# An attention block with a routed feed-forward layer on one core: the routing cut into three parts instead of two, and the attention step put in another sequence

## The reference

```python
xn = ln(x, g_norm)
q = (xn @ Wq).reshape(b, n, HEADS, DIM_HEAD).transpose(0, 2, 1, 3)
...
sim = jnp.einsum('bhid,bjd->bhij', l2norm(q) * q_scale, l2norm(k) * k_scale) * SCALE + attn_bias   # causal, masked
attn = jax.nn.softmax(sim, axis=-1)
out = jnp.einsum('bhij,bjd->bhid', attn, v)
y = ln(out.transpose(0, 2, 1, 3).reshape(b, n, HEADS * DIM_HEAD) @ Wout, g_out)
...
logits = y @ wr.T + rb
scores, idx = jax.lax.top_k(softmax(logits), 2)          # two of seven, weights normed to 1
out = expert(y, shared)
for e in range(7): out = out + w[..., e:e + 1] * expert(y, e)   # expert: (silu(y @ g.T) * (y @ u.T)) @ d.T
return x + out
```

## Time and profile before

| | us |
|---|---|
| median of 3 runs (433.98, 434.51, 672.77) | 434.51 |
| the profiled execution | 434.13 |
| its span, first to last instruction | 432.0 |
| PE, DVE, ACT, POOL busy | 357.3, 292.6, 279.5, 229.2 |
| a step of the attention, t = 3 to 14 | 12.04 |
| first send to the first routed tile's first matmul | 45.1 |
| first routed tile to the end of the span | 109.6 |

### The profile page before, as it was taken

The page is one execution under the profiler, slowest core; times in us unless marked ns, Lnnn a source line. Parts: engine busy times, 40 slices in busy tenths (PEclk is TensorE's granted clock), DMA queues, the critical chain, the costliest instruction groups (busy, mean ns, idle before and its releaser), DMA issues.

```text
span 432.0 us, 10178 instructions
## 1 busy us (share of the span) xinstructions
PE 357.3 (83%) x2921; PEld 295.1 (68%) x2922; DVE 292.6 (68%) x1144; ACT 279.5 (65%) x935; POOL 229.2 (53%) x253
## 2 busy tenths in 40 slices
PE   0286776999999999999998989697619999999980
PEld 0275655677777777777776648496519999999980
DVE  1848385888888888888889894757305565566545
ACT  1385594999999999999996773464304444444440
POOL 5024843678876667667872552277730444344420
PEclk9998995999999999999999687869958999999997
DMA  6726299990000000000000000011121222111117
GB/s 185 204 80 200 67 212 191 202 163 2 2 2 2 3 2 2 3 0 2 3 2 2 1 2 0 14 50 58 49 56 26 63 61 61 49 56 55 35 58 236
DMA packets 39479, 26.55 MB, mean 61 GB/s; under 512 B 4464, under 2 KB 37130, under 8 KB 39438
## 3 DMA queue, kind: packets, MB, share of 16 engines
q1 hardware_dynamic: 34256, 20.60, 21.8%
q0 software_dynamic: 2240, 4.23, 2.9%
q10 hardware_dynamic: 2942, 1.21, 1.1%
HBM read 12.89 MB, written 13.54 MB: 61 GB/s over the span
## 4 chain that ended last, share of the span: by engine, by line
PE 60%; DVE 16%; POOL 7%; issue 7%; ACT 5%; DMA 4%; SPq 1%; ACTq 0%; DVEq 0%; POOLq 0%
PE bank L1188 45%; PE bank L1185 14%; POOL sent_rows L537 7%; DVE p_space L1014 2%; ACT p_space L687 2%; DMA q_space<-in_L_cond_g_dram 2%; DVE biasm_space L1140 1%; DVE xn L934 1%; DMA bias<-result_rows 1%; DVE low L1018 1%; DVE p_space L841 1%; ACT xn L610 1%; DVE GL L918 1%; ACT yh L779 1%; DVE norm_in L812 1%
## 5 line engine op out<-in xcount | busy, mean ns | idle before, releaser
L687 ACT ACTIVATE p_space<-p_space,low 128x129 f32<-128x129 f32 x256 | 99.0, 391 | 6.4 <-DVE low L1018 6.4
L502 POOL TENSOR_TENSOR p_space<-p_space,inv 128x516 f32<-128x516 f32 x64 | 67.1, 1049 | 66.1 <-DVE inv L1026 66.1
L1014 DVE SCALAR_TENSOR_TENSOR p_space<-bank,rn,biasm_space 128x129 f32<-128x129 f32 x256 | 72.0, 343 | 22.3 <-PE bank L1188 22.0
L493 POOL TENSOR_TENSOR biasm_space<-bias,madd 128x516 f32<-128x516 f32 x64 | 75.6, 1192 | 7.4 <-DVE p_space L1014 7.3
L543 POOL DMA_INDIRECT result_rows<-oT_space,dest_ring x38 | 37.6, 990 | 60.8 <-DVE dest_ring L1154 60.1
L768 ACT ACTIVATE biasm_space<-bank 128x384 f32<-128x384 f32 x54 | 26.6, 492 | 58.1 <-PE bank L1185 58.0
L1185 PE MATMUL bank<-ident,p_space 128*128 128x128 f32 (+1 forms) x272 | 48.5, 297 | 2.4 <-POOL p_space L502 2.1
L687 ACT ACTIVATION_READ_ACCUMULATOR p_space<-p_space,low 128x1 f32 x256 | 48.5, 190 | 0.0
L1188 PE MATMUL bank<-DT,biasm_space 128*128 (+1 forms) x324 | 46.4, 281 | 1.2 <-ACT biasm_space L768 1.2
L702 ACT ACTIVATE pT<-bank 128x512 f32<-128x512 f32 x64 | 37.3, 583 | 13.9 <-PE bank L1188 12.8
L1018 DVE TENSOR_REDUCE low<-p_space 128x4 f32<-128x516 f32 x64 | 44.2, 691 | 2.2
(11 more groups left out here) (217 smaller groups left out, 705.4 us busy)
## 6 DMA issues: line engine op xcount, KB each, us to landing
sent_rows<-fill_row SPq DMA_DIRECT2D x2, 1950.0 KB, 24.1
sent_rows<-fill_row SPq DMA_DIRECT2D x2, 1885.0 KB, 19.6
q_space<-sent_rows SPq DMA_DIRECT2D x38, 65.0 KB, 1.9
xs<-in_x_dram SPq DMA_DIRECT2D x4, 256.0 KB, 6.3
bias<-bias_rows SPq DMA_DIRECT2D x1, 1024.0 KB, 5.8
xn<-result_rows SPq DMA_DIRECT2D x4, 256.0 KB, 4.4
bias<-result_rows SPq DMA_DIRECT2D x4, 256.0 KB, 5.6
out_dram<-xs SPq DMA_DIRECT2D x4, 256.0 KB, 2.5
```

The source lines that it names most:

```text
L493: nc.gpsimd.tensor_tensor(biasm[:, b % 2, heads, :], bias[:, heads, :], madd[:, b:b + 1, :].to_broadcast([P, HC, KEYS]), ALU.add).then_inc ...
L502: nc.gpsimd.tensor_tensor(v, v, spread(inv[:, b % 2, heads], KEYS), ALU.mult).then_inc(p_normed, 1)
L687: last = nc.scalar.activation(v, v, ACT.Exp, bias=low[:, b % 2, h:h + 1], accum_out=den[:, b % 2, h:h + 1])
L1014: last = nc.vector.scalar_tensor_tensor(Pb[:, q, h, :], src, rn[:, q, h:h + 1], biasm[:, q, h, :], ALU.mult, ALU.add)
```

## The change

1. The routing goes in three parts, of eight, four and four batches. Part 0 is normed in steps 13 and 14 and chosen, ranked and shared out in step 17; part 1 is normed in steps 15 and 16, chosen in step 17 and ranked in step 18; part 2 takes the place that the second part had among the tiles. `root_y` now runs three times instead of twice.
2. PE's step has another sequence: `mix(2)` moves from the end of a step to the next one, beside `mix(3)`; `scores(3)` moves up beside `scores(2)`; `turn_pn` goes ahead of `turn_p(3)`. The null key's matmul becomes 128 rows deep, with zeros in the 112 new rows (two more fills in the prologue).
3. The first `keep_oT` of a batch moves from ACT to DVE, between `invert(1, 1)` and `scores(3)`, and the next `mix` waits for it by a semaphore of its own. `keep_q(1)` changes places with `keep_pT(1)`, and `keep_pn` with `keep_pT(3)`, on ACT.
4. POOL's step has another sequence, with `add_mask` of chunks 3, 2 and 1 behind `norm_p(1)`.

```diff
-    PARTS = (range(0, Y_FIRST), range(Y_FIRST, NB))
+    PARTS = (range(0, NB - 8), range(NB - 8, NB - 4), range(NB - 4, NB))
...
@@ POOL, step
                 norm_p(2, 3)
-                add_mask(2, 2)
+                norm_p(3, 3)
+                norm_p(0, 2)
                 add_mask(0, 0)
-                norm_p(3, 3)
-                add_mask(3, 2)
-                norm_p(0, 2)
+                norm_p(1, 2)
+                add_mask(3, 1)
+                add_mask(2, 0)
                 add_mask(1, 0)
-                norm_p(1, 2)
...
-            pool.wait_ge(y_normed, Y_FIRST // 4)
-            nc.gpsimd.tensor_copy(send[0][0][:, :, 0:D], y_sb[:, 0:Y_FIRST, :]).then_inc(send_made[0][0], 1)
+            pool.wait_ge(y_normed, PARTS[0].stop // 4)
+            nc.gpsimd.tensor_copy(send[0][0][:, :, 0:D], y_sb[:, 0:PARTS[0].stop, :]).then_inc(send_made[0][0], 1)
...
@@ ACT, step
-                keep_oT(1, 3)
+                keep_oT()
...
+                keep_q(1)
                 keep_pT(1)
-                keep_q(1)
                 square_q(1)
...
+                if t == NB:
+                    keep_yT(0)
                 if t == NB + 1:
-                    for g in range(Y_FIRST // 4):
-                        keep_yT(g)
+                    stage(0, 1)
+                    keep_yT(2)
                 keep_pT(2)
+                if t == NB + 1:
+                    weigh(0)
                 exp(1, 1)
+                if t == NB:
+                    keep_yT(1)
                 keep_sums()
...
-                keep_oT(0, 2)
+                keep_pn()
                 keep_pT(3)
-                keep_pn()
...
@@ DVE, step
+                def keep_oT():
+                    if on(2):
+                        b = t - 2
+                        dve.wait_ge(mixed, NCH * b + 2)
+                        need(dve, y_made, b - 1)
+                        nc.vector.tensor_copy(oT[:, p, 0:HALF * P].rearrange("p (k s) -> p k s", k=HALF),
+                                              bank[6][:, :].rearrange("p (k s) -> p k s", k=HALF)[:, :, ::-1]).then_inc(oT0_kept, 1)
...
                 scores(0)
...
+                invert(3, 2)
                 scores(1)
-                invert(3, 2)
...
                 if t == NB + 1:
-                    dve.wait_ge(router_turned, 1)
...
-                if t == NB + 2:
                     choose(0)
                     mark(0)
                     rank(0)
                     share_out(0)
+                if t == NB + 2:
+                    rank(1)
+                    share_out(1)
                 keep_y()
+                if t == NB + 1:
+                    choose(1)
+                    mark(1)
...
+                keep_oT()
                 scores(3)
...
+                if t == NB - 3:
+                    root_y(0)
                 if t == NB - 2:
-                    gather_y(Y_FIRST - 1)
-                    root_y(0)
+                    scale_y(0)
+                    scale_y(1)
                 if t == NB - 1:
-                    scale_y(0)
+                    root_y(1)
                 if t == NB:
-                    scale_y(1)
                     scale_y(2)
...
@@ PE, step
+                if t == NB + 1:
+                    logits(0)
+                    logits(1)
                 if t == NB + 2:
-                    count(0)
+                    count(1)
                 queries(0)
                 turn_p(0)
+                mix(2, 3)
                 mix(3, 3)
...
                 project()
                 if t == NB + 1:
-                    for g in range(Y_FIRST // 4):
-                        logits(g)
+                    count(0)
+                    logits(2)
                 turn_p(2)
                 mix(0, 2)
                 scores(2, 1)
+                scores(3, 1)
                 mix(1, 2)
...
+                turn_pn()
                 turn_p(3)
-                scores(3, 1)
                 turn_sums()
...
-                turn_pn()
-                mix(2, 2)
```

More of the change, by code:

```diff
@@ L169, in rows_in_tile @@
             return tile[:, :, :].rearrange("p a b -> p (a b)")[:, 0:n * ROW].rearrange("p (b c) -> p b c", c=ROW)
-        send = ((rows_in_tile(bias, Y_FIRST), rows_in_tile(madd, Y_FIRST)),
-                (shared(p_space, 0, NB - Y_FIRST, ROW), shared(p_space, (NB - Y_FIRST) * ROW, NB - Y_FIRST, ROW)))
+        send = tuple(tuple(rows_in_tile(tile, PARTS[1].stop)[:, PARTS[k].start:PARTS[k].stop, :] for tile in (bias, madd))
+                     for k in range(2)) + (
+                tuple(shared(p_space, m * len(PARTS[2]) * ROW, len(PARTS[2]), ROW) for m in range(TOP)),)
         whole = (shared(p_space, H * KEYS + (NB + 1) * DH, 2, I), shared(biasm_space, (NB + 1) * 2 * DH, 2, I))
@@ L205, in adaln_ffn_kernel, with run_end @@
         placed = shared(o_space, 7 * NB * NE, TOP, NB, NE)
-        run_up = (shared(o_space, 9 * NB * NE, 2, PADS[0] + Y_FIRST, NE), shared(o_space, 12 * NB * NE, 2, PADS[1] + NB - Y_FIRST, NE))
+        RUNS = [2 * (PADS[k] + len(PARTS[k])) * NE for k in range(len(PARTS))]
+        run_up = tuple(shared(o_space, 9 * NB * NE + sum(RUNS[0:k]), 2, PADS[k] + len(PARTS[k]), NE) for k in range(len(PARTS)))
+        assert sum(RUNS) <= 4 * NB * NE
+        def run_end(k):
+            return run_up[k][:, SIDES[k], PADS[k] + len(PARTS[k]) - 1, :]
         tiles_up = shared(o_space, 13 * NB * NE, 2, EPAD + NE)
@@ L286, in run_steps, with logits_at, count_at @@
                 step(t, t % 2, lambda k, t=t: 0 <= t - k < NB)
[L288 to L294, removed]
+        y_bank = (4, 4, 2, 6)
+        def logits_at(k):
+            at = (3, 5, 6)[k], (2 * P, 0, 0)[k]
+            return bank[at[0]][:, at[1]:at[1] + NB * NE].rearrange("p (b e) -> p b e", b=NB)
+        def count_at(k, m):
+            first = (0, 0, 2 * P)[k] + m * P
+            return bank[(3, 3, 6)[k]][:, first:first + len(PARTS[k]) * NE]
         def turned_bank(t, c):
@@ L654, in keep_yT, with stage @@
                 nc.scalar.activation(YT[:, g * 512:(g + 1) * 512], bank[y_bank[g]][:, :], ACT.Copy).then_inc(yT_kept, 1)
+            def stage(k, m):
+                act.wait_ge(biasm_first, 2 * NB)
+                act.wait_ge(biasm_made, 2 * NB)
+                act.wait_ge(y_normed, PARTS[k].stop // 4)
+                nc.scalar.activation(send[k][m][:, :, 0:D], y_sb[:, PARTS[k].start:PARTS[k].stop, :],
+                                     ACT.Copy).then_inc(send_made[k][m], 1)
             def weigh(k):
@@ L719, in step @@
                 if t == NB + 2:
-                    weigh(0)
+                    weigh(1)
                 keep_q(0)
@@ L755, in _ @@
             run_steps(act, step)
-            act.wait_ge(biasm_first, 2 * NB)
-            act.wait_ge(biasm_made, 2 * NB)
-            act.wait_ge(y_normed, Y_FIRST // 4)
-            nc.scalar.activation(send[0][1][:, :, 0:D], y_sb[:, 0:Y_FIRST, :], ACT.Copy).then_inc(send_made[0][1], 1)
+            for m in range(TOP):
+                stage(1, m)
             def step(u, m, lap, kind):
@@ L787, in between @@
                 if u == 1:
-                    keep_yT(Y_FIRST // 4)
+                    keep_yT(3)
                 if u == 2:
                     for m in range(TOP):
-                        nc.scalar.activation(send[1][m][:, :, 0:D], y_sb[:, Y_FIRST:NB, :], ACT.Copy).then_inc(send_made[1][m], 1)
+                        stage(2, m)
                 if u == 3:
-                    weigh(1)
+                    weigh(2)
             run_tiles(act, step, between)
@@ L1281, in logits @@
             def logits(g):
-                pe.wait_ge(router_kept, 1)
+                k = max(k for k in range(len(PARTS)) if 4 * g >= PARTS[k].start)
+                pe.wait_ge(biased, NCH * NB)
                 pe.wait_ge(yT_kept, g + 1)
                 for b in range(4 * g, 4 * g + 4):
-                    last = mm(bank[logit_bank(b)][:, b * NE:(b + 1) * NE], YT[:, b * P:(b + 1) * P], router_wT[:, 0:NE], True, True)
-                if 4 * g + 4 in (Y_FIRST, NB):
+                    last = mm(logits_at(k)[:, b, :], YT[:, b * P:(b + 1) * P], router_wT[:, 0:NE], True, True)
+                if 4 * g + 4 == PARTS[k].stop:
                     last.then_inc(logits_made, 1)
```

115 lines of the change are left out of this document (63 added, 52 removed).

## The result

The changed kernel takes **446.19 us** (median; 445.29 to 447.20) beside 434.25 us of the kernel before on the same chip: ratio 1.028, 95% interval 1.024 to 1.032. One slow execution of the kernel before, 672.77 us, is left out of the ratio. The changed kernel is slower by 2.8%; the forecast was 444, in a range of 419 to 453. The profiled execution took 445.31 us, its span 443.3 us; before it was 432.0.

A forecast was written before the change was run, and what follows sets the result against it. PE was taken to bound the attention and POOL's sends the stretch after it. 434.1 + 16 (last row maximum later) - 6.7 (earlier routing) = 443.4, with a little for TensorE's clock 444 us; range 419 to 453.

The forecast's parts named there:

- POOL decides, against the change: Steady attention steps: three add_mask behind norm_p(1) hold up DVE's norms; step 12.8 us, 0.76 more, +9 us over twelve steps.
- PE's 1.2 us less: PE's attention step: six fewer changes of matmul shape at 0.2 us each, so its step could be 10.8 us.
- DVE's 11.25 us: DVE's need in an attention step: 10.65 us of own work plus 0.60 for the copy, making DVE the limit, not PE.
- rival 1: Steady steps: norms is not held up, the step is DVE's 11.3 us, time 422 us (415 to 428); chance 0.30.
- Steps 0 to 2, +4: First attention steps: more POOL instructions in a row block more DVE links; +4 us, between 0 and +6.
- The tail, +3: Steps 13 to 16: DVE's extra norming of the output, the copy and the router's weights; +3 us, between 0 and +5.
- TensorE's clock: Steady steps: PE's 2 us stops lower its clock, half the steps losing about 1 us; 453 us (450 to 462), chance 0.11.
- rival 3: Steady steps: PE standing still before project lowers TensorE's clock, +6 us or more, 453 us (450 to 462); chance 0.11.
- The routing, -6.7: Last row maximum to first send: 13.8 us in place of 20.5, so -6.7 us, between 0 and -10.
- The start and the end, 0: Prologue and what follows the first send: the two new fills cost nothing, the 45.1 and 109.6 us are not touched.

## Why the prediction was right, point by point

- **POOL decides, against the change**: shown, by doing and undoing it. The forecast step was 12.8 us, the measured one 12.77, and the mechanism is the forecast one: one link through for each gap. By the end of the third `add_mask` four links are through (the three of the forecast and L1080 ahead of them) and eight follow at 0.21 us.
- **PE's 1.2 us less**: the step of PE did get shorter, by less: 0.95 us for six changes, 0.16 each in place of 0.2. The 0.2 came from one pair of neighbours in which one change was seen.
- **DVE's 11.25 us, "not PE the limit, but DVE"**: wrong. DVE needs 10.87 us, and without the blocking PE is the limit at 11.09. The working took only the three long waits, 1.39 us, off the 12.04 us. By the windows DVE is busy for 10.07 us of a step, so another 0.58 us are idle in short pieces, and all of them were counted as DVE's own need. The copy itself was priced well: in the step of the changed kernel it takes 0.66 us and the next instruction begins 0.58 after it. In rival 1, which leaned on this term, the step would have been 11.1 us and the time, with the tail as it is, about 423.
- **Steps 0 to 2, +4**: +5.0, within its bounds of 0 to 6.
- **The tail, +3**: the term that was mis-sized. Beside two steps' 1.5 us it was +7.1, outside its bounds of 0 to 5. The forecast counted DVE's own instructions and not who waits for them: `turn_y(0)` has an engine of its own stand still until L1088 is through. The order showed that wait; I priced "the router's weights" as one short instruction on DVE. 4.3 us of the 7.1 go with L1088 moved, which leaves 2.8, near the forecast's 3.
- **TensorE's clock**: rival 3 did not happen where it was put. PE stands still for 1.4 us in each steady step, and the granted clock stays at 1.00. It did happen in step 16, behind the stop of 4.89 us. Its sentence that shorter waits show no such thing misread the kernel before: there the clock is at 0.50 from 238 to 242 us, behind stops of 1.11 and 1.61 us.
- **The routing, -6.7**: measured -6.7, but by two errors that cancel. `choose(0)` began 279.56 - 276.61 = 2.95 us after the maximum and not 4.5, and from there to the first send it took 10.83 us and not 9.3: POOL's last `norm_p` and its copy behind it each stretched one small DVE instruction, to 0.82 and 0.94 us, and DVE waited 1.85 us for `count(0)`. That the three parts are the cause was read from the trace; no run has them alone. The kernels with two parts have 18.4 to 20.5 us there, those with three 12.5 to 15.3 us.
- **The start and the end, 0**: -1.2 and -1.7 us. `norms` of step 0 lies between 51.0 and 54.4 us over the thirteen traces, so the first says nothing. The end takes 153.3 to 154.6 us in the three kernels with two parts and 151.4 to 153.7 in those with three, so some of the 1.7 may belong to the third part; no run tells.
- The sum came out 2 us low, since the tail was 4 dearer while the start and the end gave back 2.9. That it came so near is in part luck: without what the start and the end gave back it would have been 5 low.

The Trainium skill (SBUF — State Buffer, Who interferes with whom) would have the one that starts first hold the other out. The trace agrees for DVE, and by its number not for POOL: three `add_mask` with links between them take 3.50 us, 1.17 each, and two without took 2.34. So the step is 12.77 and not 13.1.

## What to carry to other kernels

A chain of short dependent DVE instructions on SBUF costs far more than its own time when POOL has a backlog over it: place POOL's free work so that its queue runs dry before the chain begins, and count that in microseconds from the trace, since here a second `add_mask` behind the last `norm_p` was the difference between nothing and 0.7 us a step. When a step is moved, follow each semaphore that its instructions release, however short they are: an instruction of 0.2 us held up another engine for 4.9. An edit that makes one engine's sequence better can be lost to another edit of the same change, so undo the parts one by one: here all of the change but POOL's sequence was worth 2.3%, and that one part turned it into a loss.

## What the runs showed of the hardware

- POOL lost no time to the DVE instructions that it held up: 1.17 us for an `add_mask` with and without them.
- Padding a PE operand from 16 to 128 rows with zeros made the step shorter by 0.34 and 0.35 us, in two kernels: the deeper operands did not cost more than the padding gave.
- A stop of PE of 1.4 us in every 12.8 left the granted clock at 1.00; after one of 4.9 us it was 0.50 for the 3.6 us that followed. In the kernel before it was 0.50 for 4 us behind stops of 1.11 and 1.61 us.
